# A Mamba block inside a four-layer network: where the product that feeds the scan takes its input from, and where it stands among the scans

## The reference

```python
def step(h, inp):
    dt_t, x_t, B_t, C_t = inp
    da = jnp.exp(dt_t[..., None] * A)
    h = da * h + (dt_t * x_t)[..., None] * B_t[:, None, :]
    y = jnp.einsum('bdn,bn->bd', h, C_t)
    return (h, y)
```

## Time and profile before

| | before |
|---|---|
| median of 3 runs | 3743.62 us |
| profiled execution, first to last instruction (span) | 3742.5 us |
| PE, DVE, ACT, POOL busy, share of the span | 86%, 75%, 67%, 52% |
| Mamba recurrence (first `make_u` to last scan) | about 1138 to 2308 us |
| `make_u`, 42 instructions | 594 ns shortest, 1186 median, 2160 longest |

### The profile page before, as it was taken

The page is one execution under the profiler, slowest core; times in us unless marked ns, Lnnn a source line. Parts: engine busy times, 40 slices in busy tenths (PEclk is TensorE's granted clock), DMA queues, the critical chain, the costliest instruction groups (busy, mean ns, idle before and its releaser), DMA issues. The chain is left out here.

```text
span 3742.5 us, 70954 instructions
## 1 busy us (share of the span) xinstructions
PE 3205.8 (86%) x21002; PEld 1807.7 (48%) x21002; DVE 2806.7 (75%) x4339; ACT 2516.9 (67%) x4557; POOL 1935.3 (52%) x1754
## 2 busy tenths in 40 slices
PE   5799999989787899999999867887999968788877
PEld 2588888864333444444444322333334324377742
DVE  2566666658636999999999997785999968644467
ACT  4455555548676998989998743785767638644456
POOL 0233333323246888889898875333777763200035
PEclk9899999999898999999999999998999989899999
DMA  4100000012256566574747542220000002230022
GB/s 97 30 15 14 14 15 14 14 26 52 71 168 170 144 182 188 160 209 142 211 138 208 140 120 60 56 55 23 21 22 20 20 24 51 72 70 17 17 53 61
DMA packets 211925, 297.93 MB, mean 80 GB/s; under 512 B 68990, under 2 KB 189106, under 8 KB 211382
## 3 DMA queue, kind: packets, MB, share of 16 engines
q1 hardware_dynamic: 204254, 286.98, 28.5%
q10 hardware_dynamic: 7512, 9.16, 0.9%
HBM read 193.93 MB, written 102.03 MB: 79 GB/s over the span
## 5 line engine op out<-in xcount | busy, mean ns | idle before, releaser
L1773 POOL TENSOR_TENSOR mam_hc<-mam_h,mam_cs 128x896 f32<-128x896 f32 x336 | 703.4, 2094 | 166.8 <-DVE mam_h L1692 93.5
L1692 DVE TENSOR_TENSOR_SCAN mam_h<-mam_a,mam_kept,mam_dbx 128x448 f32<-128x448 f32 x672 | 738.3, 1129 | 41.9 <-ACT mam_a L1562 40.9
L1415 PE MATMUL mam_ps_y<-mam_hc,mam_ident 128*128 128x448 f32 x1344 | 569.6, 557 | 125.2 <-POOL mam_hc L1773 124.9
L1562 ACT ACTIVATE mam_a<-mam_ft,mam_a_neg 128x448 f32<-128x448 f32 x672 | 410.8, 660 | 76.7 <-DVE mam_h L1692 75.6
L1415 PEld LDWEIGHTS mam_ps_y<-mam_hc,mam_ident 128*128 128x128 f32 x1344 | 248.5, 192 | 424.7 <-POOL mam_hc L1773 216.2
L792 POOL TENSOR_TENSOR att_prob<-att_prob,att_share 128x588 f32<-128x588 f32 x128 | 151.7, 1185 | 452.1 <-DVE att_share L977 452.1
L1679 DVE TENSOR_TENSOR mam_dbx<-mam_ps_u,mam_bs 128x448 f32<-128x448 f32 x672 | 381.3, 612 | 0.0
L2196 POOL TENSOR_TENSOR scan_ch<-scan_h,scan_cs 128x392 f32<-128x392 f32 x192 | 262.1, 1379 | 61.9 <-DVE scan_h L2138 57.5
L366 POOL TENSOR_TENSOR all_x<-all_x,f_yb 128x392 f32<-128x392 f32 x128 | 128.0, 1000 | 237.2 <-DVE f_yb L321 237.2
L360 POOL TENSOR_TENSOR all_x<-all_x,f_mixed 128x392 f32<-128x392 f32 x128 | 152.5, 1191 | 181.8 <-DMA f_mixed<-mixed 123.6
L912 ACT ACTIVATE att_pt<-att_ps_t 128x512 f32<-128x512 f32 x128 | 76.5, 598 | 209.9 <-PE att_ps_t L853 209.9
(11 more groups left out here) (252 smaller groups left out, 7870.8 us busy)
## 6 DMA issues: line engine op xcount, KB each, us to landing
mam_taps<-normed SPq DMA_DIRECT2D x220, 130.5 KB
mam_bs<-dram_bc SPq DMA_DIRECT2D x56, 448.0 KB, 8.8
mam_cs<-dram_bc SPq DMA_DIRECT2D x56, 448.0 KB, 12.0
mam_ft<-dram_steps SPq DMA_DIRECT2D x42, 448.0 KB, 4.8
normed<-f_staged SPq DMA_DIRECT2D x384, 38.1 KB
f_mixed<-mixed SPq DMA_DIRECT2D x384, 36.8 KB
mam_gt<-dram_gs SPq DMA_DIRECT2D x48, 224.0 KB, 2.7
dram_gs<-mam_gs SPq DMA_DIRECT2D x47, 224.0 KB, 2.6
```

Source lines behind the costliest of these rows:

```text
L1415: mm = pe.matmul(ps_y[p % 2][:, 0:MT], ident[:], hc[t % 2][:, i, :], start=False, stop=(t % 8 == 7 and i == 1))
L1562: act.activation(a[t % 3][:, i, :], ft[p % 2][:, 0, :], ACT.Exp, scale=a_neg[:, at:at + 1]).then_inc(decays, 1)
L1692: dve.tensor_tensor_scan(h[:, n % 8, :], a[t % 3][:, i, :], dbx[:, i, 0:MT], kept[:, at:at + 1], ALU.mult, ALU.add).then_inc(scanned, 1)
L1773: pool.tensor_tensor(hc[t % 2][:], h[:, row:row + 2, :], cs[:, 2 * pair:2 * pair + 2, :], ALU.mult).then_inc(weighed, 1)
```

## The change

ScalarE copies `x` into `ps_u` (`copy_x`), and VectorE's `make_u` multiplies `ps_u` by `dt` in place. `make_u` moves from between the two scans of a pass's last step to behind the second. `copy_x(p)` waits for the last `drive` of the pass before, and it stands in ScalarE's list behind `decay(8p + 1)`; the one of pass 0 stands ahead of `decay(0)`.

```diff
+                def copy_x(p):
+                    act.wait_ge(ft_in[p % 2], 16 * (p // 2 + 1))
+                    reached(act, driven, 16 * p)
+                    act.activation(ps_u[:, 0:MT], ft[p % 2][:, 1, :], ACT.Copy
+                                   ).then_inc(x_copied, 1)
...
                         t = 6 * j + k + 2
+                        if t == 0:
+                            copy_x(0)
                         if 0 <= t < STEPS:
                             decay(t)
+                        if t > 8 and t % 8 == 1 and t < STEPS:
+                            copy_x(t // 8)
...
                 def make_u(p):
-                    dve.wait_ge(ft_in[p % 2], 16 * (p // 2 + 1))
-                    reached(dve, driven, 16 * p)
-                    dve.tensor_tensor(ps_u[:, 0:MT], ft[p % 2][:, 0, :], ft[p % 2][:, 1, :],
+                    dve.wait_ge(x_copied, p + 1)
+                    dve.tensor_tensor(ps_u[:, 0:MT], ps_u[:, 0:MT], ft[p % 2][:, 0, :],
                                       ALU.mult).then_inc(u_made, 1)
...
                         scan(t, 0)
-                    if t % 8 == 7 and p + 1 < PASSES:
-                        make_u(p + 1)
                     if t % 8 == 3 and p > 0:
                         times_z(p - 1)
                     if t < STEPS:
                         scan(t, 1)
+                    if t % 8 == 7 and p + 1 < PASSES:
+                        make_u(p + 1)
```

More of the change, by code:

```diff
@@ L1111, in mamba_phase @@
              "skipped", "accumulated"))
+        x_copied = buf.sem("x_copied")
         (silu_a, silu_b, silu_m, silu_z, absed, relued, exped, excess, lned, bc_copied, yi_copied,
```

## The result

The changed kernel takes 3809.7 us (median of 4 runs), the kernel before 3746.6 in the same comparison: ratio 1.016, interval 1.0138 to 1.0182. The sign was forecast. The size was not: 63 us instead of 39, and 3809.7 lies above the upper end of 3804. The profiled execution's span went from 3742.5 to 3810.9 us.

The account below looks back on a forecast made before the run. ScalarE was taken as the bound in passes 10 to 33, VectorE in the three periods ahead. Early periods 11.9, later ones with stage starts 25.6, first passes 1.5: +39 us, about 3783 us; range 3760 to 3804.

Parts of the forecast that it names:

- the tie at the product: VectorE may not start pass p until ScalarE has passed decays of 8p + 1 and the copy; before, only 8p.
- Seen from ScalarE it is the same: Later period, 87.0 us, counted on ScalarE: its own 82.2, copies 1.5, plus new waits for VectorE.
- The product: VectorE's 42 products fall from 1198 to 612 ns, 24.6 us; 5.5 come back; net 19 us saved if nothing else held it.
- The copy: Each copy takes 0.5 us of ScalarE's time (0.43 to 0.56), three a period, 1.5 us on a full engine.
- The place: VectorE idle at product 6.0, 1.9, 0.3 us by pass remainder; later period 87.0 for 82.2, early 84.6 for 80.65.
- Starts of a stage: Waits for late taps at four stage starts, 18.8 us, partly covered by the new waits; 6 kept, bounds 0 and 18.8.
- Start and end of the recurrence: First copy ahead of the first decays and idle time at pass 1 cost 1.5 us; from pass 34 on, 0.
- C: Rival: nothing is covered, and ScalarE's waits for TensorE grow by 1.7 us a period, 14 in all: 3810; chance 0.12.
- its other two terms: In the 3810 rival: tap waits at stage starts stay whole, +13 us, and ScalarE's lateness counts in full.
- A: Rival: VectorE is the bound throughout, so all 19 us of shorter products come: 3725; chance 0.07.
- B: Rival: only the copies' own time counts, 12 us less about 4 of shorter products: +8, 3752; chance 0.07.

Follow-up runs that it names:

- copy_aside: Kernel before plus the 42 copies on ScalarE at the changed kernel's places, into a spare bf16 tile nobody reads: 3750.3 us, ratio 1.0008.
- pe_kept_busy: Changed kernel plus six zero-weight matmuls on TensorE behind `skip` in each pass divisible by 3: 3789.3 us, ratio 1.0115.
- link_only: Changed kernel with the copy one column wide into a spare tile; product reads both operands from SBUF but still waits for it: 3811.9 us, ratio 1.0163.
- move_only: Kernel before with only the product moved behind the second scan, both operands in SBUF, no copy: 3743.2 us, ratio 0.999; rerun 3746.6 us, 0.9995.

## Why the prediction was wrong

The forecast mechanism, the tie at the product, was right and carries two thirds of the loss. What failed is one step: "Seen from ScalarE it is the same: its own 82.2, 1.5 for copies, and waits for VectorE that it didn't have". It took ScalarE's waits for TensorE as given, because ScalarE comes to them later. It didn't follow VectorE's idle time further, through GpSimd to TensorE, and didn't ask what TensorE's clock does behind a gap of 5 us. In the period of passes 21 to 23 ScalarE's waits for TensorE went from 4.6 us to 7.8, and they are 5.0 with the clock kept up. In passes 1 to 33 the kernel before had a half clock three times, each time at the start of a stage; it is why the later periods have 0.99 in the earlier trace rows. TensorE at the start of stage 2, before:

```profile
1483.09 1.77 PE L1415 MATMUL mam_ps_y<-mam_hc,mam_ident 128*128 128x448 f32 x4 [0.85 <-POOL mam_hc L1773]
...
1489.54 3.33 PE L1362 MATMUL mam_ps_a<-mam_taps,mam_win 120*128 120x448 f32 x4 [3.78 <-DMA mam_taps<-normed]
1492.65 3.14 PE L1415 MATMUL mam_ps_y<-mam_hc,mam_ident 128*128 128x448 f32 x4
```

Point by point:

- **The product**: priced at 612 ns, measured 622. Right. What the shorter product is worth beside the waits for the tie, no run singles out.
- **The copy**: priced at 0.5 us (0.43 to 0.56), 0.53 in the trace. Its effect on the time was taken as 1.5 us a period, and none could be measured where nothing waits for the copy (copy_aside). ScalarE had 5.9 us of idle time in the period, which I had counted as part of its list.
- **The place**: waits of 6.0, 1.9 and 0.3 us were forecast for the later periods, 6.15, 2.46 and 0.0 are there; early 4.5, 1.0 and 0 against 4.65, 2.03 and 0. (VectorE's 17.0 us in the first case add up to 16.9 from their own terms.) With the clock kept up an undisturbed period is 87.7 us (forecast 87.0) and the early ones take 255.4 (forecast 253.8).
- **The clock**: not in the sum. The difference between the changed kernel and pe_kept_busy is 6.7 us in the early periods and 16.6 in the later ones; the medians differ by 20.4. This is the missed part. Without it the forecast, 3783, is 6 us from the measured 3789.3. That it comes so near is partly luck: the period was taken 0.7 us too short, 5 us over eight, and the next term 6 too long.
- **Starts of a stage**: I kept 6 of 18.8 us. In pe_kept_busy 8 x 87.7 = 701.6 is the whole of its 701.4: they are covered fully.
- **Start and end of the recurrence**: 1.5 us forecast. Measured +3.65 from the first activation to the product of pass 1 and -1.5 behind pass 34, so 2.1 together.
- **The range**: the bounds of the parts together give 3766 to 3805, where 3760 to 3804 was stated; the clock wasn't among the parts.

Of the rivals, C named the result, 3810, and had 0.12. Its part "its waits for TensorE grow as the engines are bound closer" is what happened, priced at 1.7 us a period where the clock cost 2.1 (16.6 by 8); but its other two terms did not occur, so its number is right partly by chance. A and B fell. Their common premise, that a full engine sets the time, was also mine for ScalarE in passes 10 to 33, and copy_aside took it away.

What would have given the number: the forecast of VectorE's 6 us stall, then the question which engine is fed by it. The rows above, from the trace of the kernel before, already show a step's two matmuls at 3.14 us behind a gap of 3.78, instead of 1.77.

## What to carry to other kernels

A semaphore from one engine's list to another's cost here what the two lists differ by at that place, not what the instruction costs that carries it: the same copy one step earlier in ScalarE's list left +0.2% of the +1.6%. When a stall of some microseconds is forecast, follow it to the engines fed by the stalled one, down to TensorE: here such a gap was paid twice, since the work behind it ran on half the clock. And a busy engine is a bound only where a run shows it: in the early periods 3.9 us less of VectorE's time made 3.6, but in the period of 82.2 us, where all four engines are 90% busy or more, 0.9 us more on ScalarE and 2.0 less on TensorE changed nothing, and 2.0 more on TensorE made 1.2.

## What the runs showed of the hardware

- TensorE's granted clock was 0.50 behind stretches of 6 us in which it had been busy for about 1 us, once a period, and a step's two matmuls of 128x448 took 3.35 us there instead of 1.67. Six matmuls with zero weights in the gap kept it at 1.00 and made the kernel 20 us faster. Without its `skip` matmuls the kernel before had the clock at 0.98 in two of three undisturbed periods, and those took 83.8 and 83.9 us, against 82.2 in the third at 1.00.
- The same product took 622 ns on average with one operand in PSUM, and 941 and 955 with both in SBUF (link_only, move_only), where it can lie beside a GpSimd product. At the place between the scans it had been 1198.
- ScalarE's copy of 128x448 f32 from SBUF to PSUM took 528 ns, and 562 from SBUF to a bf16 tile in SBUF.
